# Split operands for an output projection, two linear sums side by side, one buffer per tile, and the last unit's denominators on TensorE

## The reference, cut to what matters

```python
Q, K, V = (q @ Wq.T + bq), (k @ Wk.T + bk), (v @ Wv.T + bv)       # q = x, k = v = ctx
att = softmax(Q @ K.T / sqrt(32))                                  # per head, 1024 x 1024
out = (att @ V) @ Wo.T + bo                                        # the output projection
x1  = layernorm(out + q, gamma0, beta0)
Q_phi, K_phi = elu(x1), elu(ctx)
KV = einsum('bnd,bne->bde', K_phi, ctx)                            # the linear sums
Z  = 1 / (einsum('bnd,bd->bn', Q_phi, K_phi.sum(axis=1)) + 1e-6)
y  = layernorm(x1 + einsum('bnd,bde->bne', Q_phi, KV) * Z[..., None], gamma1, beta1)
```

## Time and profile before

| | us |
|---|---|
| median of three runs | 1528.52 |
| lowest, highest | 1524.69, 1529.03 |
| the profiled execution, whole | 1526.61 |
| its span, first to last instruction | 1525.2 |
| PE, DVE, POOL, ACT busy in it | 1481.1, 1297.9, 1237.8, 826.7 |

### The profile page before, as it was taken

How to read it: one execution, slowest core, us unless ns; L and a number is a source line. 1 busy time by engine, 2 the same in 40 slices (tenths; PEclk the granted TensorE clock), 3 DMA queues, 4 the chain that set the end, 5 groups by cost and what they waited for, 6 DMA issues and landing times.

```text
span 1525.2 us, 30133 instructions
## 1 busy us (share of the span) xinstructions
PE 1481.1 (97%) x10528; PEld 1043.0 (68%) x10528; DVE 1297.9 (85%) x2509; ACT 826.7 (54%) x1595; POOL 1237.8 (81%) x1100
## 2 busy tenths in 40 slices
PE   8999999999999999999999999999999999999886
PEld 6767767676767777667676767666767667756554
DVE  6687888778898988987898897989789889988886
ACT  2454655555555555665555555655555555555542
POOL 0486787767899898967888898877889898897995
PEclk9999999999999999999999999999999999999998
DMA  7744254433325244243344326235242434410001
GB/s 223 212 134 135 70 161 128 148 110 111 111 85 149 79 130 148 77 127 120 96 126 128 104 85 179 91 101 141 87 130 86 145 112 116 130 51 27 7 22 42
DMA packets 159574, 170.14 MB, mean 112 GB/s; under 512 B 20288, under 2 KB 122048, under 8 KB 159424
## 3 DMA queue, kind: packets, MB, share of 16 engines
q1 hardware_dynamic: 157696, 167.16, 36.7%
q10 hardware_dynamic: 1728, 1.05, 0.2%
HBM read 125.97 MB, written 42.21 MB: 110 GB/s over the span
## 4 chain that ended last, share of the span: by engine, by line
PE 83%; DVE 5%; POOL 5%; issue 3%; DMA 2%; ACT 1%; SPq 1%; POOLq 0%; DVEq 0%; ACTq 0%
PE score L465 15%; PE scoreT L479 14%; PE acc L497 13%; PE misc L540 7%; PE misc L552 7%; PE misc L516 7%; PE misc L529 7%; PE misc L577 6%; PE misc L569 4%; POOL pair_sum L1044 2%; PE acc L506 2%; DVE maxes L778 1%; DVE pair_sum L818 1%; POOL pair_sum L1053 1%; PE misc L560 1%
## 5 line engine op out<-in xcount | busy, mean ns | idle before, releaser
L643 ACT ACTIVATE p_ring<-scoreT 128x512 f32<-128x512 f32 x1024 | 597.6, 595 | 552.2 <-PE scoreT L479 546.3
L1044 POOL TENSOR_TENSOR pair_sum<-p_ring 128x512 f32<-128x512 f32 x512 | 665.5, 1308 | 173.1 <-ACT p_ring L643 106.9
L778 DVE TENSOR_REDUCE maxes<-score 128x1 f32<-128x512 f32 x1024 | 678.8, 678 | 114.9 <-PE score L465 108.7
L465 PE MATMUL score<-k_stack,q_stack 96*128 96x512 f32 x1024 | 601.9, 589 | 6.8 <-DVE maxes L778 5.1
L479 PEld LDWEIGHTS scoreT<-q_stack,k_stack 104*128 104x128 f32 x2048 | 390.0, 192 | 155.9 <-ACT p_ring L643 80.1
L479 PE MATMUL scoreT<-q_stack,k_stack 104*128 104x256 f32 x2048 | 421.9, 288 | 7.1 <-ACT p_ring L643 6.6
L465 PEld LDWEIGHTS score<-k_stack,q_stack 96*128 96x128 f32 x1024 | 193.5, 189 | 164.4 <-issue 101.5
L1053 POOL TENSOR_TENSOR pair_sum<-pair_sum 128x512 f32<-128x512 f32 x192 | 253.3, 1319 | 0.0
L497 PE MATMUL acc<-p_ring,v_sb 128*32 128x256 f32 x4096 | 250.1, 385 | 0.0
L818 DVE TENSOR_TENSOR pair_sum<-pair_sum 128x512 f32<-128x512 f32 x192 | 216.7, 1129 | 5.8 <-POOL pair_sum L1044 5.8
L497 PEld LDWEIGHTS acc<-p_ring,v_sb 128*32 128x32 f32 x4096 | 120.8, 110 | 85.4 <-issue 3.5
(11 more groups left out here) (95 smaller groups left out, 1361.8 us busy)
## 6 DMA issues: line engine op xcount, KB each, us to landing
xT_sb<-xT_in SPq DMA_DIRECT2D x63, 512.0 KB, 3.9
q_stack<-q_dram SPq DMA_DIRECT2D x189, 128.0 KB, 2.5
k_stack<-k_dram SPq DMA_DIRECT2D x93, 256.0 KB, 4.4
ctx_nat<-ctx_in SPq DMA_DIRECT2D x32, 256.0 KB, 4.2
q_dram<-q_high SPq DMA_DIRECT2D x63, 128.0 KB, 1.7
q_dram<-q_low SPq DMA_DIRECT2D x63, 128.0 KB, 1.9
k_dram<-k_high SPq DMA_DIRECT2D x31, 256.0 KB, 2.0
k_dram<-k_low SPq DMA_DIRECT2D x31, 256.0 KB, 2.2
```

The costliest lines, as they stand in the source:

```text
L465: pe.matmul(score[k % 3][:], q_stack[0:SPLIT, unit % NQ, j, t * P:(t + 1) * P], k_stack[0:SPLIT, group_of[unit] % 2 * QUAD + j, h * HALF:( ...
L643: act.activation(p_ring[:, n % NP, h * HALF:(h + 1) * HALF], scoreT[k % 2][:], ACT.Exp, scale=SCALE).then_inc(A["exped"], 1)
L778: dve.reduce_max(maxes[:, unit % 2, t, j, h:h + 1], score[k % 3][:], AX.X).then_inc(V["maxed"], 1)
L1044: pool.tensor_tensor(pair_sum[:, place_of_pair(pair), cols], p_ring[:, (n - 1) % NP, cols], p_ring[:, n % NP, cols], ALU.add).then_inc(L[" ...
```

## The change

It has five parts. (1) The output projection takes split operands: ACT copies a tile's `outT` to `o_high` and DVE subtracts to get `o_low`, six and five ticks ahead of the O chain; `wo` is split once. Each of the four pieces of O is now three products. `outT` has five places for groups in turn, so that for batches 1 to 3 the copy and the subtraction of a tile each take two instructions (128 and 384 columns, or twice 256). (2) S handles two blocks side by side: 16 pieces, two per context tile, in both `misc` banks; the features are made 256 columns wide, in place, and the context tiles stream through four buffers, loaded again for the second pair of blocks by ACT's queue. (3) A tile has one buffer for x, y and the result instead of two, there are four in turn instead of three, and the last eight tiles have their own. The features of a tile are reduced in place after they were turned. (4) The last unit has no pair sums: 16 products of `ones` with `p_ring` are added to each of its two visits. (5) The planner's numbers change with all this; its last tick is 1114 instead of 1103.

```diff
-    NQ, NP, NO, NX = 3, 7, 19, 3
+    NQ, NP, NO, NX, NCTX = 3, 7, 5, 4, 4
+    EXTRA, LAST_SLOTS = 8, [NX, NX + 1, NX + 2, NX + 3, NX + 4, NX + 5, NX + 6, NX + 7]
+    S_FIRST, S_GAP = 52, 96
+    SPLIT_LEAD, S_PAUSE = 6, 3
+    SUMMED = UNITS - 1
...
-        LENGTH = {"K": 4, "V": 4, "Q": 2, "O": 4, "T": 1, "A": 4, "S": 8, "N": 1, "B": 4}
+        LENGTH = {"K": 4, "V": 4, "Q": 2, "O": 4, "T": 1, "A": 4, "S": 16, "N": 1, "B": 4}
...
-            return max(UT * unit_at[G * b + G - 1, t // TPC] + LEAD + 28, spaced if b < B - 1 else 0)
+            return max(UT * unit_at[G * b + G - 1, t // TPC] + LEAD + 27 + SPLIT_LEAD, spaced if b < B - 1 else 0)
...
+                if unit >= SUMMED:
+                    for s in range(VISIT):
+                        n = VISIT * v + s
+                        for j in range(QUAD):
+                            mm = pe.matmul(acc[j * DK:(j + 1) * DK, CH:2 * CH], ones[:],
+                                           p_ring[:, n % NP, j * CH:(j + 1) * CH], start=False,
+                                           stop=n % KT == KT - 1, tile_position=(0, j * DK), skip_group_check=True)
                 mm.then_inc(T["weighted"], 1)
-                if part < KT // VISIT - 1:
+                if unit >= SUMMED or part < KT // VISIT - 1:
                     return
...
-                    pe.wait_ge(V["out_scaled"], unit_at[G * b + G - 1, t // TPC] + 1)
+                    pe.wait_ge(V["o_low_kept"], tile + 1)
                     if tile == 0:
-                        pe.wait_ge(M["wo"], 16)
-                mm = pe.matmul(bank_of("O", tile)[:], outT[:, unit % NO, t % TPC * P:(t % TPC + 1) * P], wo[:, g, :],
-                               start=g == 0, stop=g == G - 1)
+                        pe.wait_ge(V["wo_low_kept"], G)
+                for term, (part, wo) in enumerate(((o_high, wo_high), (o_high, wo_low), (o_low, wo_high))):
+                    mm = pe.matmul(bank_of("O", tile)[:], part[place_of_tile(tile)][:, g, :], wo[:, g, :], start=g == 0 and term == 0,
+                                   stop=g == G - 1 and term == 2)
...
+            def sum_kv(i, piece):
+                t, d = divmod(piece, 2)
+                step = KT * i + t
+                if d == 0:
+                    pe.wait_ge(V["f_phi"], step + 1)
+                pe.matmul(bank_of("kv", 2 * i + d)[:], fphi_sb[:, step % NPHI, d * P:(d + 1) * P],
+                          ctx_nat[:, step % NCTX, :], start=t == 0, stop=t == KT - 1).then_inc(T["kv_piece"], 1)
...
+            def keep_o_high(tile):
+                b, t = divmod(tile, KT)
+                last = unit_at[G * b + G - 1, t // TPC]
+                act.wait_ge(V["out_scaled"], last + 1)
+                if tile == TILES - KT + 1:
+                    act.wait_ge(M["k_out1"], landed_keys(GROUPS - 1, 1, 2))
+                elif tile >= 1:
+                    act.wait_ge(T["o_projected"], tile - (tile > TILES - KT))
+                for gs, places in runs_of_places(b):
+                    copy = act.activation(o_high[place_of_tile(tile)][:, gs, :],
+                                          outT[:, places, t // TPC, t % TPC * P:(t % TPC + 1) * P], ACT.Copy)
+                copy.then_inc(A["o_high_kept"], 1)
...
+            def context_features(step):
+                cols = slice(step // KT % 2 * CH, (step // KT % 2 + 1) * CH)
+                act.wait_ge(M[f"ctx{step % NCTX}"], landed(step, NCTX, 1))
+                if step >= NPHI:
+                    act.wait_ge(T["kv_piece"], 2 * (step - NPHI + 1))
+                    i, before = divmod(step - NPHI, KT)
+                    act.wait_ge(L["totalled"], (KT - 1) * i + max(before, 1))
+                f = fphi_sb[:, step % NPHI, :]
+                act.activation(f, ctx_nat[:, step % NCTX, cols], ACT.Relu, scale=-1.0).then_inc(A["f_below"], 1)
+                act.wait_ge(A["f_below"], step + 1)
+                act.activation(f, f, ACT.Exp, scale=-1.0).then_inc(A["f_grown"], 1)
+
+            def load_context(step):
+                b, t = step // (2 * KT), step % KT
+                act.wait_ge(T["kv_piece"], 2 * (step - NCTX + 1))
+                act.dma_start(ctx_nat[:, step % NCTX, :], ctx[b, t * P:(t + 1) * P, :]
+                              ).then_inc(M[f"ctx{step % NCTX}"], 16)
...
+            def keep_o_low(tile):
+                b, t = divmod(tile, KT)
+                dve.wait_ge(A["o_high_kept"], tile + 1)
+                for gs, places in runs_of_places(b):
+                    part = outT[:, places, t // TPC, t % TPC * P:(t % TPC + 1) * P]
+                    low = dve.tensor_tensor(o_low[place_of_tile(tile)][:, gs, :], part,
+                                            o_high[place_of_tile(tile)][:, gs, :].bitcast(F32),
+                                            ALU.subtract)
+                low.then_inc(V["o_low_kept"], 1)
...
-                out=x_nat[slot_of[tile]], in0=e_sb[:, tile % 2, :], in1=phi_total[:], scale=1.0, scalar=0.0,
+                out=e_sb[:, tile % 2, :], in0=e_sb[:, tile % 2, :], in1=phi_total[:], scale=1.0, scalar=0.0,
...
-                if 0 <= pair < KT * UNITS // 2 and i < 2:
+                if 0 <= pair < RUN_PAIRS * SUMMED and i < 2:
                     add_pair(pair, i)
```

More of the change, by code:

```diff
@@ L350, in follow @@
             if kind == "S":
-                if i % G == G - 1 and i < G * (B - 1):
-                    for t in range(0, KT, 2):
-                        send("ctx", end + 2 + t, KT * (i // G + 1) + t, 2)
                 for k in range(start_of["S", i], end + 1):
-                    if k in pieces and pieces[k][0] == ("S", i):
-                        take("ACT", k - 4, 5)
-                        take("DVE", k - 3, 5)
-                        take("POOL", k - 2, 5)
+                    chain, piece = pieces.get(k, (None, 0))
@@ L359, in follow @@
+                    if chain == ("S", i) and piece % 2 == 0:
+                        take("ACT", k - 4, 8)
+                        take("DVE", k - 3, 8)
+                        take("POOL", k - 2, 8)
+                    elif chain == ("S", i) and KT * i + piece // 2 + NCTX < KT * 2 * B:
+                        when.setdefault("context", {})[k + 2] = KT * i + piece // 2 + NCTX
+                        take("ACT", k + 2, 4)
             elif kind == "O":
+                for name, engine, ahead in (("o_high", "ACT", SPLIT_LEAD), ("o_low", "DVE", SPLIT_LEAD - 1)):
+                    when.setdefault(name, {})[start_of["O", i] - ahead] = i
+                    take(engine, start_of["O", i] - ahead, 7)
@@ L365, in follow @@
             elif kind == "T":
-                if i + 1 in grow_of:
-                    make_features(i + 1)
+                if ("N", i // KT) in end_of:
+                    dot_of[i] = book("dot", "DVE", max(end, end_of["N", i // KT] + 1) + 1, 13, i)
+                else:
+                    undotted.append(i)
+                if i in dot_of and i + 2 in normed_of:
+                    make_features(i + 2)
+            elif kind == "N":
+                for tile in undotted:
+                    dot_of[tile] = book("dot", "DVE", end + 2, 13, tile)
+                    if tile + 2 in normed_of:
+                        make_features(tile + 2)
+                undotted.clear()
@@ L405, in build @@
                     k += 1
+                if chain[0] == "S" and piece == 2 * NCTX:
+                    k += S_PAUSE
                 while visiting(k) is not None:
@@ L1237, in load_x @@
                     sp.wait_ge(M[f"out{s}"], landed_tile(before[tile]))
+                if before[tile] < 0 and slot_of[tile] < NX:
+                    sp.wait_ge(V["wo_low_kept"], G)
                 if slot_of[tile] >= NX:
```

286 lines of the change are left out of this document (152 added, 134 removed).

## The result

The changed kernel takes 1540.67 us (median of 4 runs, 1538.88 to 1543.04), the kernel before 1526.61 beside it (1524.66 to 1529.03). The ratio is 1.0089, with a 95% interval of 1.0073 to 1.0105: slower by 0.9%, where I had forecast 1.3% faster. The profiled execution took 1542.27 us, its span is 1541.0, against 1525.2 before.

The account below looks back on a forecast made before the run. PE was taken to set the pace (97% busy), with DVE and POOL close behind. Gains of 19.2 + 2.7 + 2.6 + 5 less losses of 3 + 4 + 1 made 21.5 us, so a median of 1507 us, own range 1499 to 1515.

Parts of the forecast that it names:

- the new plan, with the sums and the last unit: All terms without the split: 2.7, 2.6 and 5 us gained, 3 and 1 lost, a gain of 6.3 us.
- `o_low` on DVE: Splits in stretches with O: 47 us of DVE time, fitting on average, taken as 4 us lost for the program.
- three products in place of fp32: Output projection on PE: each of 128 O pieces saves 0.15 us, 19.2 us gained; called the safest term.
- the bare ticks: Ticks 26 to 1024: 155 bare ticks instead of 151, some in runs of seven where maxima outlast PE; 1 us lost.
- DVE above 97%: Sign of being wrong: DVE busier than 97% between O and A pieces.
- The linear sums: S pieces keep their length; stalls near 1341 and 1412 us and DVE's short waits shrink, 5 us gained (0 to 12).
- The end: Last 45 us: 2.7 us net from removed pair sums, 2.6 from the clock, 3 lost to DVE's order.
- The bound of 3.4 us a tile: Upper bound of split time on DVE, each of a pair waiting for one whole POOL instruction; 1.8 us lost per stretch.
- DVE saturated, and PE's clock with it: Rival: at 3.4 us a tile DVE is short and PE's clock falls, 1528 to 1536 us; chance 0.07.
- DVE takes over: Rival, stretches with O: PE's 19.2 us partly or wholly return as waits, 1517 to 1526 us; chance 0.2.
- The signs: Right: 1.18 us O ticks, no end `pair_sum` wait, 1.6 us pairs, fewer stops; wrong: maxima waits, DVE above 97%, clock under 0.95.

Follow-up runs that it names:

- e3: The kernel after with the output projection in plain fp32 again and nothing split, order of work as after: 1537.8 us, ratio 1.0071 to before.
- e2: The kernel after without the `o_low` subtraction, the third product reading `o_high` instead (wrong result, only time used): 1527.2 us, ratio 0.9992 to before.
- e9: The kernel after with plain fp32 output projection, its planner freed of the split's lead, O spacing and booked time: 1523.7 us, ratio 0.9985 to before.
- e12: The kernel after with GpSimd waiting for its own last instruction before each bo or beta addition and gamma multiplication: 1534.4 us, ratio 1.0047 to before.
- e7: The kernel before, own plan, each O piece as three fp32r products of an unsplit operand (wrong result, only time used): 1515.6 us, ratio 0.9927 to before.
- e18: The kernel after with plain fp32 O, planner freed of the split, and the last unit's denominators from sums again: 1528.9 us, ratio 1.0002 to before.
- e1: The kernel after with `o_low` copied on DVE instead of subtracted (wrong result, only time used): 1535.7 us, ratio 1.0047 to before.
- e4: The kernel after with the `o_low` subtraction on GpSimd instead of DVE, at the same ticks: 1551.9 us, ratio 1.0160 to before.

## Why the prediction was wrong

The forecast was 21.5 us of gain, the measurement 13.6 of loss, 35.1 apart. Three steps failed.

| | forecast | measured | apart |
|---|---|---|---|
| the new plan, with the sums and the last unit (e3) | 6.3 gained | 10.8 lost | 17.1 |
| `o_low` on DVE (e2 to after) | 4 lost | 14.8 lost | 10.8 |
| three products in place of fp32 (e3 to e2) | 19.2 gained | 12.0 gained | 7.2 |

The measured column adds up by the way it is made, each row from one kernel to the next.

The largest failure is a term put at next to nothing without a reason: the order of work. Of the plan I had counted the bare ticks ("I put 1 us on it") and nothing else. The split's rules in it, six ticks of lead and one O chain waiting for the one before, cost 13.1 us (e3 to e9) with no split at all in the kernel. In the profiled pair some two thirds of it were stalls and the rest came behind the last score, once the pieces that moved are counted out; which instruction's wait each tick of lead lengthens stays open.

The second is the price of the split on DVE: "It fits on average, but the maxima have only three score buffers of slack, so bunches will stop PE", and then "take 4 us for the whole program". Measured: 14.8 us, 15.6 without long holds. The durations came out longer too. I had 1.13 us for one instruction, 1.6 for a pair and 47 us in all; the kernel after has 1.77, 2.24 and 67.9 (56 instructions of L935), e12 has 0.97, 1.87 and 52.8. But the 4 us weren't worked out from the 47: what was wrong is the rule by which time on DVE becomes time of the program. I let it cost nothing until DVE is full, and so named "DVE above 97%" as the sign. DVE was at 93%, and each microsecond on it cost some 0.2 to 0.4 us (14.8 of 67.9, 15.6 of 52.8, 6.4 of the 17.1 that the copy saves).

- *The products.* Right in size per piece (1.17 us a tick) and wrong as a sum: 11 to 12 us, not 19.2. All but the last tiles' pieces were to lie on the path, "since PE is what bounds there". Of the 16.5 us that came off e7's floor a third came back as stalls, and the 20 pieces behind the last score gave nothing. That the shorter ticks ask DVE for maxima sooner fits (PE's wait for them rose from 5.1 to 6.5 us in e7), but is only part of the 6.1.
- *The linear sums.* 5 us of gain forecast; e18 shows none. DVE had 12% more room there, but PE hadn't been waiting in those stretches. The place that the 5 us were read from still costs a stop of 1.84 us and a spell at the lower clock. The relief was in one place and the new load in another.
- *The end.* The wait of 5.34 us is gone, the twelve products of A take 2.75 us as forecast (2.8), the clock is 0.95 over the last 88 us. Yet the time behind the last score is no shorter. I forecast 3 us of loss from DVE's order and missed the plan's: O of tile 24 begins at tick 992 in place of 985, the last store stands at 1112 in place of 1101, and 59 pieces in place of 55 remain behind the last score. e9, whose plan ends at 1099, has 76.9 us there.
- *The bound of 3.4 us a tile.* I let an instruction wait for one POOL instruction. Four instructions waited for three each, and the end of a fourth. (14.1 - 2.4 - 13.6 is also 1.9 and not 1.8; nothing hangs on it.)
- *The rivals.* "DVE saturated, and PE's clock with it", at 7%, is the one that came nearest in time (1528 to 1536), and its picture is right at three of the four long holds of `o_low`, with the lower clock behind them; behind the first, at 431.6 us, the clock didn't fall. As an account of the whole it is wrong, and that its time is the nearest is luck: `o_low` took 2.1 us a tile on average and not 3.4, cost 14.8 us and not 25, with DVE at 93% in the stretch read, and half of the miss was the plan. Nor does its 1536 follow: 0.3 us more for each of 32 tiles is 9.6 us, so 1538, or 1545 at its ratio of 1.8. "DVE takes over" names the right wait, PE's for the maxima, but leaves a gain, 1517 to 1526, since it too has no term for the plan.
- *The signs.* Of those of being right two came (1.17 us a tick, no wait for `pair_sum` at the end), the pairs at 1.6 us and the fewer stops did not. Of those of being wrong the first came, PE waiting for row maxima (22.5 us); DVE stayed under 97% there, and the clock was 0.99 (425 to 566 us) and 1.00 (610 to 700 us).

By experiment, then: products -12.0, `o_low` +14.8, plan with plain O and the cheaper last unit +10.8, together +13.6. Why a tick of lead more or less costs what it does (the end, or the ticks at which POOL's runs meet DVE's instructions) was not taken apart further.

The Trainium skill, "SBUF — State Buffer", section "SBUF: two separate sides", says that the one of the two engines that starts first has the port pair for its whole instruction and that the other "fully blocks"; and that a copy in a two-port mode takes the same lock as an instruction with two SBUF inputs. The traces agree that each holds the other for whole instructions, the copy too (4.04 us in e1); in which mode the copy ran no trace shows. The traces show besides that the one who waits can lose again at the next boundaries, two of them at 524.30 us.

## What to carry to other kernels

Give a change of the plan a term of its own: here the order of work that the split asked for cost 13 us, about as much as the subtractions themselves (15). When one engine is at 97% and its partner at 90%, price work on the partner from the first microsecond (here 0.2 to 0.4 us each), not from the point where its busy share is full, and count of a faster piece on the bounding engine only the part that its suppliers can follow (here 12 of 19 us). Look for relief where the bounding engine waits, not where a busy share is high. Where two engines shut each other out, look at the order of both: a wait of the one on its own last instruction gave 6 to 9 us in the new plan, and nothing in the old one, which had hardly any long holds.

## What the hardware showed

- A DVE instruction whose operands are in SBUF can be held over three GpSimd instructions that follow one another without a gap: 4.3 us for some 0.7 of work (5.7 us over five in e4, two of them of 0.7 us). All instructions of 3.9 us and more in the kernel after began within 0.1 us of the end of a GpSimd instruction; in e3 one of 3.9 us began 0.36 us behind one.
- Waits of GpSimd on its own last instruction end this, at 10 us more of GpSimd's busy time (1218.2 to 1228.6), and the program gets 6.4 us faster (after to e12).
- It goes both ways: in e12's trace GpSimd's own instructions of 1.27 us take 1.70 to 1.74 where DVE was first.

```profile
522.64 1.52 DVE L935 TENSOR_TENSOR o_low<-outT,o_high 128x512 fp32r<-128x512 f32 x1
...
525.28 0.68 DVE L904 TENSOR_TENSOR pair_sum<-pair_sum 128x512 f32<-128x512 f32 x1
...
523.57 1.74 POOL L1165 TENSOR_TENSOR pair_sum<-pair_sum 128x512 f32<-128x512 f32 x1
525.38 1.70 POOL L1198 TENSOR_TENSOR tiles<-tiles,beta_row 128x512 f32<-128x512 f32 x1
```

- In the kernel after PE's stops of 2.92 us (to 529.96) and 1.79 us (to 807.57) were each followed by 3.4 us at the lower clock, 1.2 GHz, from 531.5 and from 808.0; a stop of 1.72 us (to 437.18) was followed by none.
